# Graph network with expert layers: row sums to three tables, pair adds moved, more key codes joined

## The chip, the cores and the metric

The kernel runs on one core of a Trainium2 chip. The metric is the device time of one execution in microseconds. Three executions of the kernel before took 6115.59 to 6121.12 us, median 6119.78.

## The reference

A table x of 2500 nodes by 256 features passes through eight residual blocks, each on a layer norm of x: an edge network (GIN) with edge features, an expert layer, a graph convolution, an expert layer, a convolution with attention, an expert layer routed by attention over a second graph, an attention block over the first graph, and a last expert layer. The edges of the first list (42500) and of the second (131072) are given as index arrays.

```python
# first block
msg = relu(x[src] + edge_attr @ We + be)          # 42500 x 256
agg = segment_sum(msg, dst, num_segments=2500)
out = (x + agg) @ W + b                           # then batch norm, relu
# graph convolution
out = segment_sum((x @ W)[src] * norm[:, None], dst)
# sixth block
e = leaky_relu(a_src[src] + a_dst[dst]); ee = exp(e - segment_max(e, dst)[dst])
```

## The kernel before, in words

The five compute and queue programs (SP loads, PE, DVE, ACT, POOL) are written out by hand, with semaphores between them. SP, PE, ACT and DVE go through the stages together: each ends a stage in `stage_end` and goes on when all four are there. POOL has no stages. It runs `edges_pool` and then `pairs_pool` straight through, and is tied to the others by semaphores only.

The sums over edges are made in two ways. The first block adds rows: the edges of the first list are taken in K1 = 340 tiles of 125. For tile k POOL gathers the source rows from DRAM (`gather`, L809), PE multiplies the edge features and adds the gathered rows (L632), ACT takes the relu, DVE builds a matrix that sums the tile's edges of equal target (L725), PE multiplies by it (L599), ACT keeps the result (L669), and POOL adds its rows to a table in DRAM by an indirect DMA with addition (`add`, L822). Two edges of a tile with one target are summed before, so an indirect add never meets a row twice; adds to the same table must not be in flight together. So there are two tables, `sums[k % 2]`, and the add of k waits until that of k − 2 has landed. Eight gathers run ahead. The last column of the table counts the degree.

The other blocks use a dense count table of 2500 x 2500 pairs. Each tile of edges is added to it by an indirect DMA of one element per lane (`add_pair`, L760): 340 adds for the first list (table `pairs1`), 1024 tiles of 128 for the second (two tables `pairs2`, the adds alternate between them in portions). Before a tile can be added, DVE compares its keys with those of a super-tile of four tiles (`key1_codes`, L527) so that only one edge of each key in it adds, with the count. For the second list (`key2_codes`, L545) p counts pairs of super-tiles, eight tiles each. Where `joined(p)` holds, each tile is compared over all eight (1024 wide), and the eight are added to one table as one portion. Where it doesn't, each half is compared by itself (512 wide) and portions are of four. A portion waits until the earlier adds to its table have landed.

In the edges stage DVE and PE work in 85 groups of GR = 4 tiles, and every group also codes one super-tile of the first list and, from group 1 on, one pair p of the second (`pairs_of`: groups 20, 40, 60 and 80 have two), up to p = 87. The rest are coded in the first expert stage. So p = 16 falls in group 17, p = 32 in group 32 and p = 53 in group 52.

The order of POOL's work is: adds and gathers in turn for k = 0 to 339, and from k = FIRST1 = 112 (group 28) on EARLY1 = 132 pair adds of the first list spread evenly among them (L835). Then `pairs_pool`: four adds of the first list and two of the second in turn until the first is done, then the rest of the second.

SP, in the edges stage (`edges_sp`), zeroes `sums`, then the tails of the pair tables, then loads the edge features group by group (L560) with a portion of the pair tables' zeroing behind each, and 36 parameter loads (L660) after group 79. The gin stage (`gin_sp`, L850) waits for all row sums, loads both tables back in five blocks, and DVE adds them (L870, L871). SP waits for the whole first list (`pairs_added`) before the table loads of the first graph convolution, and for the whole second list (`pairs2_added`) before those of the sixth block; the stage ahead of the latter stores expert outputs (`outs_e`).

```python
sp.wait_ge(sem("pairs_added"), 16 * K1)          # first gate
table_sp(sp, "l1g", pairs1)
...
for c in range(2):                               # second gate
    sp.wait_ge(sem(f"pairs2_added{c}"), 16 * ADDED2[c])
nbmax_ahead(sp, "l2h", pairs2)
```

Of the kernel before, what the change touches and what calls it, by code (L numbers as in the profile page):

```python
# [22 lines left out]
ALU = mybir.AluOpType  # L23
# [4 lines left out]
N, D = 2500, 256  # L28
P, T = 125, 20
E1, K1 = 42500, 340  # L30
# [8 lines left out]
AGG = D + 1  # L39
# [4 lines left out]
RANK = 1024  # L44
GR = 4
SUPER = 4


LOCAL = 40
# [5 lines left out]
def build(nc, a, out):  # L55
    ctx = ExitStack()
    with ctx:
# [3 lines left out]
        def dram(name, shape, dt=F32):  # L61
            return nc.dram_tensor(name, shape, dt, kind="Internal").ap()
# [7 lines left out]
        def sem(name):  # L70


            if name.startswith(ACROSS):
                if name not in sems:
                    sems[name] = ctx.enter_context(nc.semaphore(name))
                return sems[name]
            names = sems.setdefault(here[0], [])
            if name not in names:
                names.append(name)
            return local[names.index(name)]  # L80
# [6 lines left out]
        WORK = sb("WORK", [128, 10240])  # L87
# [26 lines left out]
        GAT = [sb(f"GAT{i}", [P, T, 4]) for i in range(8)]  # L114

        x_table = dram("x_table", [N, D])
        sums = [dram(f"sums{c}", [N + 128, AGG]) for c in range(2)]
        PAIR_OF = 2 * SUPER
        pairs1 = dram("pairs1", [PAIRS + 128 * PAIR_OF, 1])
        pairs2 = [dram(f"pairs2_{c}", [PAIRS + 128 * PAIR_OF, 1]) for c in range(2)]  # L120
# [61 lines left out]
        LOADED = 32  # L182
        LANES = (slice(0, 112), slice(112, P))

        def spread(sp, name, dst, src):

            for lanes in LANES:
                sp.dma_start(dst[lanes], src[lanes], allow_slow_non_contiguous=True).then_inc(sem(name), 16)  # L188
# [309 lines left out]

        def joined(p):

            return 16 <= p < 32 or 54 <= p < 106

        def key1_rows(pe, g):
            for part in range(3):
# [46 lines left out]
        def edges_sp(sp):  # L551
            sp.dma_start(WE[0:ED], a["L0_gnn_We"]).then_inc(sem("we_loaded"), 16)
            sp.dma_start(WE[ED:ED + 1], a["L0_gnn_be"].rearrange("(e d) -> e d", e=1)).then_inc(sem("we_loaded"), 16)
            zeros = [(table, f"zeroed{1 if table is pairs1 else 2}", at)
                     for table in (pairs1, *pairs2) for at in range(ZP)]

            def group(g):
                if g >= 2:
                    sp.wait_ge(sem("edge_added"), GR * (g - 1))
                sp.dma_start(EA_T[0:ED, g % 2, :], a["edge_t"][:, g * GR * P:(g + 1) * GR * P]  # L560
                             ).then_inc(sem(f"ea_loaded{g % 2}"), 16)

            def zero(table, name, at):
                sp.dma_start(table[0:PAIRS, :].rearrange("(r p q f) o -> r p q (f o)", r=ZP, p=ZL, q=5)[at],
                             ZERO[0:ZL, 0:PAIRS // (ZP * ZL) // 5].unsqueeze(1).to_broadcast([ZL, 5, PAIRS // (ZP * ZL) // 5])
                             ).then_inc(sem(name), 16)

            group(0)
            sp.wait_ge(sem("cleared_zero"), 1)
            for c in range(2):  # L570
                spread(sp, f"zeroed_sums{c}", sums[c][0:N, :].rearrange("(q p r) d -> p q (r d)", p=P, r=10),
                       ZERO[:, 0:10 * AGG].unsqueeze(1).to_broadcast([P, 2, 10 * AGG]))
                sp.dma_start(sums[c][N:N + 128, :].rearrange("(a p) d -> p a d", p=64),
                             ZERO[0:64, 0:2 * AGG].rearrange("p (a d) -> p a d", d=AGG)
                             ).then_inc(sem(f"zeroed_sums{c}"), 16)
            for table in (pairs1, *pairs2):
                sp.dma_start(table[PAIRS:PAIRS + 128 * PAIR_OF, :].rearrange("(p a) o -> p (a o)", p=64),
                             ZERO[0:64, 0:2 * PAIR_OF]).then_inc(sem("zeroed1" if table is pairs1 else "zeroed2"), 16)
            for g in range(1, NG):
                group(g)  # L580
                done = 3 * ZP - len(zeros)
                due = -(-3 * ZP * g // (NG - 6))
                for _ in range(min(due - done, len(zeros))):
                    zero(*zeros.pop(0))
                if g == NG - 6:
                    params(sp)
            assert not zeros
            stage_end(sp)
# [73 lines left out]
        def edges_act(act):  # L662
            act.wait_ge(sem("cleared_sums"), 1)

            def keep(k):
                act.wait_ge(sem("edge_sums"), k + 1)
                if k >= 8:
                    act.wait_ge(sem(f"rows_added{k % 2}"), 16 * ((k - 8) // 2 + 1))
                act.activation(SUMMED[0:P, k % 8, :], PS[0:P, 4 + k % 2, 0:AGG], ACT.Copy).then_inc(sem("sum_kept"), 1)  # L669

            for k in range(K1):
                act.wait_ge(sem("edge_added"), k + 1)
                if k >= 2:
                    act.wait_ge(sem("edge_sums"), k - 1)
                act.activation(MSG[0:P, k % 2, 0:D], PS[0:P, 2 + k % 2, 0:D], ACT.Relu).then_inc(sem("msg_ready"), 1)  # L675
                if k:
                    keep(k - 1)
            keep(K1 - 1)
            stage_end(act)
# [74 lines left out]
            finish(NG - 1, True)  # L754
            stage_end(dve)

        FIRST1, EARLY1 = 112, 132

        def add_pair(pool, table, done, idx, cnt, n):
            pool.indirect_dma_start(table, bass.IndirectOffsetOnAxis(idx[:, n:n + 1], 0), cnt[:, n:n + 1], None,  # L760
# [36 lines left out]
        def edges_pool(pool):  # L797
            pool.memset(ZERO[:, 0:PAIRS // (ZP * ZL)], 0.0).then_inc(sem("cleared_zero"), 1)
            pool.wait_ge(sem("cleared_zero"), 1)
            pool.memset(SUMMED[96:128], 0.0).then_inc(sem("cleared_sums"), 1)  # L800
            pool.wait_ge(sem("cleared_sums"), 1)
            pool.memset(EA_T[64:65], 1.0).then_inc(sem("cleared_ones"), 1)
            pool.wait_ge(sem("t0_stored"), NC * LOADED)

            def gather(k):

                if k >= 8:
                    pool.wait_ge(sem("edge_added"), k - 7)
                pool.indirect_dma_start(GATH[:, k % 8, :], None, x_table,  # L809
                                        bass.IndirectOffsetOnAxis(SRCI[:, k:k + 1], 0)  # L810
                                        ).then_inc(sem(f"gathered{k % 8}"), 16)

            def add(k):
                c = k % 2
                pool.wait_ge(sem("sum_kept"), k + 1)
                if k < 2:
                    pool.wait_ge(sem(f"zeroed_sums{c}"), LOADED + 16)
                if k % GR == 0:
                    pool.wait_ge(sem("rows_coded"), k // GR + 1)
                if k >= 2:  # L820
                    pool.wait_ge(sem(f"rows_added{c}"), 16 * (k // 2))
                pool.indirect_dma_start(sums[c], bass.IndirectOffsetOnAxis(SROW[:, k:k + 1], 0),  # L822
                                        SUMMED[:, k % 8, :], None, compute_op=ALU.add
                                        ).then_inc(sem(f"rows_added{c}"), 16)

            for k in range(8):
                gather(k)
            pairs = 0
            for k in range(K1):
                add(k)  # L830
                if k + 8 < K1:
                    gather(k + 8)
                if k == FIRST1:
                    pool.wait_ge(sem("zeroed1"), 16 * (ZP + 1))
                for n in range(pairs, max(0, EARLY1 * (k + 1 - FIRST1) // (K1 - FIRST1))):  # L835
                    add_pair1(pool, n)
                    pairs += 1
            assert pairs == EARLY1
# [5 lines left out]
        SUMS = [Y[:, 0:T * AGG], flat(ROWS[0:P].rearrange("p a b -> p (a b)"), T * D, T * AGG)]  # L844
        SUMS_T = [v.rearrange("p (t d) -> p t d", d=AGG) for v in SUMS]
        four = lambda c: slice(4 * c, 4 * c + 4)

        def gin_sp(sp):
            for c in range(2):
                sp.wait_ge(sem(f"rows_added{c}"), 16 * K1 // 2)  # L850
            for n in range(NC):
                for c in range(2):
                    spread(sp, f"gin_sums{n}", SUMS_T[c][:, four(n)],
                           sums[c][0:N, :].rearrange("(t p) d -> p t d", p=P)[:, four(n)])
            sp.wait_ge(sem("params_loaded"), 16 * N_PARAMS)
            stage_end(sp)

        def gin_dve(dve):

            st = Steps(dve, "gin_steps")  # L860
# [5 lines left out]
                    st.go(dve.bn_stats(BN[:, m, c * 6:(c + 1) * 6], O0[:, m, c * CH:(c + 1) * CH]))  # L866

            for c in range(NC):
                dve.wait_ge(sem(f"gin_sums{c}"), 2 * LOADED)
                st.step(dve.tensor_tensor(SUMS_T[0][:, four(c)], SUMS_T[0][:, four(c)], SUMS_T[1][:, four(c)], ALU.add))  # L870
                dve.tensor_tensor(XN[:, four(c)], XN[:, four(c)], SUMS_T[0][:, four(c), 0:D], ALU.add  # L871
                                  ).then_inc(sem("gin_in"), 1)
                if c >= 2:
                    stats(c - 2)
# [1868 lines left out]
```

## Time and profile before

| what | value |
| --- | --- |
| three runs, median | 6119.78 us |
| profiled execution, span | 6109.5 us |
| PE busy | 4932.3 us (81%) |
| DVE busy | 3794.6 us (62%) |
| POOL busy | 3155.8 us (52%) |
| ACT busy | 1630.4 us (27%) |
| L760 (pair adds) | 1364 of 1576 ns |
| L822 (sum adds) | 340 of 1562 ns |
| L809 (gathers) | 340 of 1008 ns |

The span reaches from the first to the last instruction; what the device time has beyond it lies before and after. The profile has no time of its own for the profiled execution beside the span. Busy shares are means over stages with different limits, and issuing of DMAs by SP is not counted as busy. An idle time of 0.30 us with the releaser "issue" is one in which the profile shows nothing that the engine waited for.

### The profile page before, as it was taken

Reading aid. Unit: us, or ns where it says so; the run is one execution under the profiler, and the core shown is the slowest. Engines: PE = TensorE matmul, PEld = TensorE weight load, DVE = VectorE, ACT = ScalarE, POOL = GpSimd, SP = SyncE. Lnnn points to the kernel's source line nnn. Section 1 sums busy time; section 2 is a strip of 40 time slices with the busy share of each in tenths; the row PEclk is TensorE's granted clock in tenths of the full one; section 3 lists DMA queues with packets and bytes.
Section 4 is the critical chain, followed back from the end, with each engine's and each line's share of the span. In section 5 each row is a group of like instructions: output and inputs, shape, how many; then the busy total and the mean of one; then the engine's idle time right before and its main releaser. Section 6 shows DMA issues by size and latency. Waiting matters only on the chain.

```text
span 6109.5 us, 70270 instructions
## 1 busy us (share of the span) xinstructions
PE 4932.3 (81%) x23497; PEld 2951.4 (48%) x23497; DVE 3794.6 (62%) x7229; ACT 1630.4 (27%) x2765; POOL 3155.8 (52%) x2151
## 2 busy tenths in 40 slices
PE   5766666656889898989668979777766999999999
PEld 3444444434445575557566656673223333222266
DVE  6797668876676602130234520699996998777744
ACT  2111111112112201220122222127772002666521
POOL 5678888888888888888877877002220000000000
PEclk8878777777999998999877879889998999999999
DMA  7776666665444595559798866884433011222200
GB/s 191 153 143 137 122 128 122 129 96 63 6 11 18 18 125 33 16 7 125 83 191 89 90 51 72 175 174 121 112 102 74 29 29 28 82 81 82 79 11 28
DMA packets 558594, 523.44 MB, mean 86 GB/s; under 512 B 263641, under 2 KB 489874, under 8 KB 557159
## 3 DMA queue, kind: packets, MB, share of 16 engines
q1 hardware_dynamic: 295560, 427.91, 31.5%
q0 software_dynamic: 261696, 90.13, 23.7%
q8 instruction: 164, 2.69, 0.2%
q14 instruction: 146, 1.20, 0.1%
q10 hardware_dynamic: 1028, 1.52, 0.1%
HBM read 365.58 MB, written 153.75 MB: 85 GB/s over the span
## 4 chain that ended last, share of the span: by engine, by line
PE 52%; DVE 18%; issue 9%; SPq 7%; DMA 7%; POOL 6%; ACT 1%; DVEq 0%; ACTq 0%; POOLq 0%; PEldq 0%
SPq L188 6%; PE PS L2390 6%; PE PS L1448 6%; PE PS L1057 6%; PE PS L2227 5%; PE PS L1029 5%; DVE WORK L2031 4%; DVE MXS L2268 4%; PE PS L1754 3%; PE PS L1040 3%; DVE XT L545 3%; POOL sums L822 3%; DVE ROWS L545 2%; DMA WORK<-x_table,WORK 2%; PE PS L1254 2%
## 5 line engine op out<-in xcount | busy, mean ns | idle before, releaser
L760 POOL DMA_INDIRECT pairs<-PAIR_CNT,PAIR_IDX x1364 | 2150.1, 1576 | 491.2 <-issue 453.4
L545 DVE SCALAR_TENSOR_TENSOR XT<-PS,ROWS 128x1024 f32<-128x1024 f32 (+1 forms) x704 | 694.0, 1050 | 160.1 <-PE PS L515 159.7
L822 POOL DMA_INDIRECT sums<-WORK,XT x340 | 531.2, 1562 | 169.3 <-issue 100.8
L2461 DVE SCALAR_TENSOR_TENSOR WORK<-WORK 125x1000 f32<-125x1000 f32 x400 | 462.3, 1197 | 151.1 <-ACT WORK L2429 150.4
L632 PE MATMUL PS<-WORK,IDENT 125*125 125x256 f32 x680 | 277.3, 497 | 272.7 <-DMA WORK<-x_table,WORK 272.4
L2227 PE MATMUL PS<-ROWS 32*125 32x500 f32 x3200 | 451.0, 633 | 28.9 <-DVE MXS L2268 19.3
L2268 DVE TENSOR_REDUCE MXS<-PS 125x4 f32<-125x2000 f32 x200 | 438.9, 2236 | 24.1 <-PE PS L2248 20.0
L2019 POOL TENSOR_TENSOR WORK<-WORK,ROWS 125x500 f32<-125x500 f32 x100 | 126.0, 1260 | 630.8 <-ACT WORK L1983 630.8
L2429 ACT ACTIVATE WORK<-PS 125x1000 f32<-125x1000 f32 x400 | 380.0, 1002 | 237.8 <-PE PS L2378 237.8
L675 ACT ACTIVATE WORK<-PS 125x256 f32<-125x256 f32 x340 | 131.0, 385 | 1155.0 <-PE PS L632 1155.0
L515 PE MATMUL PS<-ROWS 128*128 128x512 bf16 x768 | 265.6, 471 | 212.0 <-DVE XT L545 154.3
L1057 PE MATMUL PS<-WORK 128*125 128x256 f32 x1760 | 408.7, 387 | 3.7 <-ACT WORK L1126 3.7
L809 POOL DMA_INDIRECT WORK<-x_table,WORK x340 | 342.8, 1008 | 127.8 <-issue 87.8
L1029 PE MATMUL PS<-XT,WORK 128*128 128x500 f32 x880 | 394.5, 592 | 5.4 <-DVE X L1109 2.1
L1705 DVE CUSTOM_DVE_ANT_0 ROWS<-ROWS 125x1250 f32<-125x1250 f32 x200 | 281.0, 1458 | 189.6 <-ACT ROWS L1691 189.5
L1162 DVE SCALAR_TENSOR_TENSOR X<-PS,G,X 125x256 f32<-125x256 f32 x280 | 122.9, 479 | 443.3 <-PE PS L1057 442.9
L1057 PEld LDWEIGHTS PS<-WORK 128*125 128x125 f32 x1760 | 338.6, 193 | 90.8 <-issue 37.1
L1448 PE MATMUL PS<-Y,WORK 125*125 x1600 | 356.0, 386 | 6.7 <-DMA WORK<-pairs 6.7
L1671 PE MATMUL PS<-IDENT,WORK 125*125 125x125 f32 x1920 | 259.2, 305 | 123.0 <-ACT ROWS L1691 63.8
L1448 PEld LDWEIGHTS PS<-Y,WORK 125*125 125x125 f32 x1600 | 306.3, 192 | 61.0 <-issue 13.4
L632 PEld LDWEIGHTS PS<-WORK,IDENT 125*125 125x125 f32 x680 | 150.1, 240 | 357.2 <-DMA WORK<-x_table,WORK 333.6
L527 DVE SCALAR_TENSOR_TENSOR ROWS<-PS,WORK,XT 125x500 f32<-125x500 f32 x340 | 230.7, 735 | 137.9 <-PE PS L505 137.8
(338 smaller groups left out, 8134.3 us busy)
## 6 DMA issues: line engine op xcount, KB each, us to landing
WORK<-pairs SPq DMA_DIRECT2D x400, 218.8 KB
pairs<-ROWS SPq DMA_DIRECT2D x75, 976.6 KB, 7.4
WORK<-pairs SPq DMA_DIRECT2D x48, 1093.8 KB
WORK<-pairs SPq DMA_DIRECT2D x80, 546.9 KB
pairs<-PAIR_CNT,PAIR_IDX POOLq DMA_INDIRECT x1364
WORK<-pairs SPq DMA_DIRECT2D x40, 382.8 KB
XT<-pairs SPq DMA_DIRECT2D x12, 1093.8 KB
mask_t<-ROWS SPq DMA_DIRECT2D x40, 273.4 KB
```

Source lines behind the costliest of these rows:

```text
L188: sp.dma_start(dst[lanes], src[lanes], allow_slow_non_contiguous=True).then_inc(sem(name), 16)
L545: dve.scalar_tensor_tensor(junk[:, slot:slot + width // SUPER, :].rearrange("p a n -> p (a n)"), PS[:, bank + (0 if both else h):bank + (2 ...
L632: pe.matmul(PS[0:P, 2 + k % 2, 0:D], IDENT[0:P, 0:P], GATH[0:P, k % 8, :], start=False, stop=True).then_inc(sem("edge_added"), 1)
L760: pool.indirect_dma_start(table, bass.IndirectOffsetOnAxis(idx[:, n:n + 1], 0), cnt[:, n:n + 1], None, compute_op=ALU.add).then_inc(sem(do ...
L822: pool.indirect_dma_start(sums[c], bass.IndirectOffsetOnAxis(SROW[:, k:k + 1], 0), SUMMED[:, k % 8, :], None, compute_op=ALU.add).then_inc ...
L1029: ins = pe.matmul(PS[:, m, 0:CH], w1[:, k, m * 128:(m + 1) * 128], XT[:, k, c * CH:(c + 1) * CH], start=k == 0, stop=k == 1)
L1057: ins = pe.matmul(PS[0:P, 6 + j // 2, (j % 2) * D:(j % 2 + 1) * D], h, w3[:, k, :], start=k == 0, stop=k == kk - 1)
L1448: ins = pe.matmul(sums_of(j), TABLE_IN[u][0:P, j * P:(j + 1) * P], Y256[:, ds(i * TABLES + u, 1), :], start=False, stop=False, skip_group_ ...
L2227: ins = pe.matmul(PS[0:P, banks[g], 0:CH], HT[group(g), m, t * P:(t + 1) * P], HT[group(g), m, c * CH:(c + 1) * CH], start=True, stop=last)
L2268: dve.tensor_reduce(MXS[:, at:at + G4], PS[0:P, b:b + G4, 0:CH], AX, ALU.max).then_inc(sem("l3m_read"), 1)
L2429: act.activation(E3[q % 8], PS[0:P, b:b + 2, 0:CH], ACT.Exp, scale=float(DH) ** -0.5).then_inc(sem("l3a_exp"), 1)
L2461: dve.scalar_tensor_tensor(E3[q % 8], E3[q % 8], 1.0, A3[n % 4][0:P].unsqueeze(1).to_broadcast([P, 2, CH]), ALU.min, ALU.mult).then_inc(se ...
```

## The change

There are three tables of row sums instead of two, taken in turn; all three are zeroed at the start, and gin reads and adds three. For blocks 3 and 4 of the third table SP waits until the buffer's former block is summed. 96 instead of 132 pair adds of the first list are spread among the edges, from the same tile on; the other 36 follow in `pairs_pool`. The pairs p = 32 to 53 of the second list are joined too.

```diff
--- before.py
+++ after.py
@@ -44,6 +44,7 @@
 RANK = 1024
 GR = 4
 SUPER = 4
+N_SUMS = 3
 
 
 LOCAL = 40
@@ -114,7 +115,7 @@
         GAT = [sb(f"GAT{i}", [P, T, 4]) for i in range(8)]
 
         x_table = dram("x_table", [N, D])
-        sums = [dram(f"sums{c}", [N + 128, AGG]) for c in range(2)]
+        sums = [dram(f"sums{c}", [N + 128, AGG]) for c in range(N_SUMS)]
         PAIR_OF = 2 * SUPER
         pairs1 = dram("pairs1", [PAIRS + 128 * PAIR_OF, 1])
         pairs2 = [dram(f"pairs2_{c}", [PAIRS + 128 * PAIR_OF, 1]) for c in range(2)]
@@ -498,7 +499,7 @@
 
         def joined(p):
 
-            return 16 <= p < 32 or 54 <= p < 106
+            return 16 <= p < 106
 
         def key1_rows(pe, g):
             for part in range(3):
@@ -567,7 +568,7 @@
 
             group(0)
             sp.wait_ge(sem("cleared_zero"), 1)
-            for c in range(2):
+            for c in range(N_SUMS):
                 spread(sp, f"zeroed_sums{c}", sums[c][0:N, :].rearrange("(q p r) d -> p q (r d)", p=P, r=10),
                        ZERO[:, 0:10 * AGG].unsqueeze(1).to_broadcast([P, 2, 10 * AGG]))
                 sp.dma_start(sums[c][N:N + 128, :].rearrange("(a p) d -> p a d", p=64),
@@ -665,7 +666,7 @@
             def keep(k):
                 act.wait_ge(sem("edge_sums"), k + 1)
                 if k >= 8:
-                    act.wait_ge(sem(f"rows_added{k % 2}"), 16 * ((k - 8) // 2 + 1))
+                    act.wait_ge(sem(f"rows_added{(k - 8) % N_SUMS}"), 16 * ((k - 8) // N_SUMS + 1))
                 act.activation(SUMMED[0:P, k % 8, :], PS[0:P, 4 + k % 2, 0:AGG], ACT.Copy).then_inc(sem("sum_kept"), 1)
 
             for k in range(K1):
@@ -754,7 +755,7 @@
             finish(NG - 1, True)
             stage_end(dve)
 
-        FIRST1, EARLY1 = 112, 132
+        FIRST1, EARLY1 = 112, 96
 
         def add_pair(pool, table, done, idx, cnt, n):
             pool.indirect_dma_start(table, bass.IndirectOffsetOnAxis(idx[:, n:n + 1], 0), cnt[:, n:n + 1], None,
@@ -811,14 +812,14 @@
                                         ).then_inc(sem(f"gathered{k % 8}"), 16)
 
             def add(k):
-                c = k % 2
+                c = k % N_SUMS
                 pool.wait_ge(sem("sum_kept"), k + 1)
-                if k < 2:
+                if k < N_SUMS:
                     pool.wait_ge(sem(f"zeroed_sums{c}"), LOADED + 16)
                 if k % GR == 0:
                     pool.wait_ge(sem("rows_coded"), k // GR + 1)
-                if k >= 2:
-                    pool.wait_ge(sem(f"rows_added{c}"), 16 * (k // 2))
+                if k >= N_SUMS:
+                    pool.wait_ge(sem(f"rows_added{c}"), 16 * (k // N_SUMS))
                 pool.indirect_dma_start(sums[c], bass.IndirectOffsetOnAxis(SROW[:, k:k + 1], 0),
                                         SUMMED[:, k % 8, :], None, compute_op=ALU.add
                                         ).then_inc(sem(f"rows_added{c}"), 16)
@@ -844,13 +845,16 @@
         SUMS = [Y[:, 0:T * AGG], flat(ROWS[0:P].rearrange("p a b -> p (a b)"), T * D, T * AGG)]
         SUMS_T = [v.rearrange("p (t d) -> p t d", d=AGG) for v in SUMS]
         four = lambda c: slice(4 * c, 4 * c + 4)
+        SUMS_3 = [flat(WORK, 6200 + u * 4 * AGG, 4, AGG)[0:P] for u in range(3)]
 
         def gin_sp(sp):
-            for c in range(2):
-                sp.wait_ge(sem(f"rows_added{c}"), 16 * K1 // 2)
+            for c in range(N_SUMS):
+                sp.wait_ge(sem(f"rows_added{c}"), 16 * len(range(c, K1, N_SUMS)))
             for n in range(NC):
-                for c in range(2):
-                    spread(sp, f"gin_sums{n}", SUMS_T[c][:, four(n)],
+                if n >= 3:
+                    sp.wait_ge(sem("gin_in"), n - 2)
+                for c in range(N_SUMS):
+                    spread(sp, f"gin_sums{n}", SUMS_T[c][:, four(n)] if c < 2 else SUMS_3[n % 3],
                            sums[c][0:N, :].rearrange("(t p) d -> p t d", p=P)[:, four(n)])
             sp.wait_ge(sem("params_loaded"), 16 * N_PARAMS)
             stage_end(sp)
@@ -866,8 +870,9 @@
                     st.go(dve.bn_stats(BN[:, m, c * 6:(c + 1) * 6], O0[:, m, c * CH:(c + 1) * CH]))
 
             for c in range(NC):
-                dve.wait_ge(sem(f"gin_sums{c}"), 2 * LOADED)
+                dve.wait_ge(sem(f"gin_sums{c}"), N_SUMS * LOADED)
                 st.step(dve.tensor_tensor(SUMS_T[0][:, four(c)], SUMS_T[0][:, four(c)], SUMS_T[1][:, four(c)], ALU.add))
+                st.step(dve.tensor_tensor(SUMS_T[0][:, four(c)], SUMS_T[0][:, four(c)], SUMS_3[c % 3], ALU.add))
                 dve.tensor_tensor(XN[:, four(c)], XN[:, four(c)], SUMS_T[0][:, four(c), 0:D], ALU.add
                                   ).then_inc(sem("gin_in"), 1)
                 if c >= 2:
```

## Rows read from the trace of the kernel before

**Rows 1.** The page: span, and slices of POOL.
```profile
span 6109.5 us, 70270 instructions
...
POOL 5678888888888888888877877002220000000000
```

**Rows 2.** Busy time by stretch (start:end length, then busy us per engine).
```profile
50.00:286.00 236.00, 171.23 (x584) 116.03 (x584) 161.61 (x620) 43.58 (x132) 163.29 (x128) 0.80 0.75 164
...
850.00:1290.00 440.00, 293.78 (x910) 186.15 (x909) 368.06 (x988) 67.98 (x206) 358.92 (x267) 0.75 0.67 125
```

**Rows 3.** Groups of POOL, 850 to 1290 us (busy, mean ns | idle before).
```profile
L822 POOL DMA_INDIRECT sums<-WORK,XT x104 | 161.7, 1555 | 31.7 <-issue 29.0 <-ACT WORK L669 2.1 <-DVE XT L734 0.3
L809 POOL DMA_INDIRECT WORK<-x_table,WORK x103 | 104.6, 1015 | 31.4 <-issue 25.6 <-PE PS L632 4.3 <-DMA sums<-WORK,XT 1.5
L760 POOL DMA_INDIRECT pairs<-PAIR_CNT,PAIR_IDX x60 | 93.7, 1562 | 18.3 <-issue 17.7 <-DMA sums<-WORK,XT 0.3 <-DVE PAIR_IDX L687 0.3
```

**Rows 4.** Timeline of DVE, edges (start us, us, what).
```profile
398.37 0.34 DVE L725 SCALAR_TENSOR_TENSOR WORK<-PS,WORK 125x125 f32<-125x125 f32 x1
...
485.55 0.34 DVE L725 SCALAR_TENSOR_TENSOR WORK<-PS,WORK 125x125 f32<-125x125 f32 x1
...
1396.80 1.28 DVE L545 SCALAR_TENSOR_TENSOR XT<-PS,ROWS 128x1024 f32<-128x1024 f32 x1
...
1398.01 1.28 DVE L545 SCALAR_TENSOR_TENSOR XT<-PS,ROWS 128x1024 f32<-128x1024 f32 x1
```

**Rows 5.** Groups of DVE by form, 560 to 840 us.
```profile
L545 DVE SCALAR_TENSOR_TENSOR XT<-PS,ROWS 128x512 f32<-128x512 f32 x136 | 93.7, 747 | 49.8 <-PE PS L515 49.6
```

**Rows 6.** Source line 822 (the sum adds), 50 to 286 us.
```profile
  issue: 29.0, 44
  DMA sums<-WORK,XT: 16.8, 10
...
DMA to landing us min/median/max: 3.8/4.4/6.7
```

**Rows 7.** Timeline, start of the edges, SP and POOL.
```profile
51.82 1.61 POOL L822 DMA_INDIRECT sums<-WORK,XT  x1 [10.00 <-issue]
...
57.47 1.46 SPq L560 DMA_DIRECT2D WORK<-in_edge_t  x1
...
64.66 1.58 POOL L822 DMA_INDIRECT sums<-WORK,XT  x1 [9.92 <-DMA sums<-ROWS]
```

**Rows 8.** Timeline, end of the edges.
```profile
1322.24 59.32 SPq L560 DMA_DIRECT2D WORK<-in_edge_t  x5
...
1417.63 0.16 DVE L695 SCALAR_TENSOR_TENSOR PAIR_IDX<-ROWS,SPARES 128x8 int32<-128x8 f32 x1
...
1420.46 1.54 POOL L822 DMA_INDIRECT sums<-WORK,XT  x1 [0.30 <-issue]
...
1424.28 0.84 SPq L188 DMA_DIRECT2D Y<-sums  x2
```

**Rows 9.** Gin: a stretch as in rows 2, and DVE's timeline.
```profile
1424.00:1450.00 26.00, 12.98 (x49) 8.21 (x50) 12.20 (x12) 7.32 (x18) 18.70 (x11) 0.68 1.07 198
...
1430.86 1.23 DVE L870 TENSOR_TENSOR Y<-Y,ROWS 125x1028 f32<-125x1028 f32 x1 [13.07 <-DMA ROWS<-sums]
```

**Rows 10.** Waits on POOL, 2290 to 2616 us (us in total, times, longest).
```profile
POOL pairs L760 <- DMA pairs<-PAIR_CNT,PAIR_IDX: 8.9, 7, 2.8
```

**Rows 11.** Timeline at the two gates.
```profile
2120.17 5.44 SPq L188 DMA_DIRECT2D WORK<-pairs  x8
...
3817.21 1.54 POOL L760 DMA_INDIRECT pairs<-PAIR_CNT,PAIR_IDX  x1 [0.30 <-issue]
...
3841.01 7.72 SPq L188 DMA_DIRECT2D outs_e<-ROWS  x4
...
3851.78 15.53 SPq L188 DMA_DIRECT2D WORK<-pairs  x8
```

## The prediction

> **What bounds the kernel now.** I read the page first, then a table by stage, then each queue. The page gives a span of 6109.5 us [rows 1]; the median of the runs shown is 6119.8, 10.3 above it. The sum is made in the span's times and its difference is taken off the median. A measurement of this kernel tells 0.2% (12 us) from no change. The page shows POOL at 7 or 8 tenths for over half of the span and then idle: its indirect transfers run in one string that ends at 3817 us [rows 1, 11]. In the edges, between 850 and 1290 us, POOL is busy 358.9 of 440 us. That is saturation, because every issue is followed by 0.30 us put down to "issue" [rows 2, 3].
>
> So from tile k = 112 on a tile costs POOL a sum add (1.555 + 0.30), a gather (1.015 + 0.30) and 132/228 of a pair add (1.562 + 0.30) [rows 3]: 3.17 + 1.08 = 4.25 us, 17.0 per group of four. Check: 104 tiles in 440 us are 4.23 each. DVE is under that: where it paced the kernel, six groups of joined codes took from 398.37 to 485.55 us, 14.5 each [rows 4]. Before k = 68 no pair is joined, and POOL sets the pace with waits of its own: 64 sum adds in 236 us, 3.69 per tile against 3.17 [rows 2, 6]. Groups 17 to 27 (joined, still without pair adds) go at DVE's 14.5 against POOL's 12.7.
>
> After the edges two gates tie the other engines to POOL. SP needs the first list before the load at 2120.17, and the whole second list before the load at 3851.78. POOL issues its last pair add at 3817.21. The nearest row for a landing, that of sum adds, has a median of 4.4 us, so it is over at 3822; SP's last stores of the stage before are issued until 3848.7 [rows 6, 11]. **The second gate has 30 us of slack, and on that number this change turns.**
>
> **36 pair adds out of the edges.** Each is 1.86 us, 36 make 67 us. On POOL nothing is saved: they come later in the same string. For the other engines the edges end sooner, as long as POOL stays the bound: a tile costs 3.17 + 96/228 × 1.86 = 3.95 us, a group 15.8, against DVE's 14.5 in every group from 28 on, since groups 32 to 52 are joined as well. Groups 40, 60 and 80 code two pairs, 8 × 1.21 = 9.7 us more (a 1024-wide code starts 1.21 us after the one before) [rows 4]. POOL does not starve on that: up to seven sums are kept and not yet added, 7 × 3.95 = 28 us of work, and DVE recovers 1.3 us a group. At the end it is tight. SP issues the 36 parameter loads and only then, from 1322 us, the last edge loads; DVE ends at 1417.8, the last sum add is issued at 1420.46, and gin's first load at 1424.28 [rows 8]. DVE's tail does not shrink, POOL's last 35 tiles do by 35 × 0.29 = 10 us, so some 5 of the 67 us are lost upstream, and POOL idles some 3 us (0 to 10).
>
> **The third table, waits.** A sum add now waits for the add three before it, not two. Up to 286 us POOL waited 16.8 us for sum adds in 10 places (13.8 over the usual 0.30). "Issue" holds 29.0 in 44 places, of which 13.2 is the usual and 9.7 the first add; the other 6 may be the same wait [rows 6, 7]. In three turns of 3.17 an add has 9.5 us to land, and the longest took 6.7 [rows 6]. I take 18 us (0 to 20). What stands between 286 and 468 us lies under DVE's pace and gives nothing.
>
> **The third table, zeroing.** 2500 × 257 × 4 bytes = 2.57 MB more are zeroed on SP's queue ahead of group 1's edge load. With two tables that load is issued at 57.47, and the add of k = 1, which waits for the second table's zeros, comes 12.8 us after that of k = 0, at 64.66 [rows 7]. I take 13 us (9 to 18) for all engines, before k = 2 and group 1. Net at the start: 18 − 13 = 5 us gained, on POOL too.
>
> The page DMA: Bandwidth & Descriptors of the Trainium skill, section Bandwidth, gives some 358 GB/s between SBUF and HBM for a core, by which the zeros would be an estimated 7 us and the final gain 6 us more. The row has 12.8 for the same size, and that stands in the sum.
>
> **The third table, reading.** Gin loads 2.57 MB more, in 30 transfers instead of 20. From 1424 to 1450 us the DMA engines were full (share 1.07) at 198 GB/s: 13 us. DVE adds once more per block, 1.23 us, of which the last is on the path [rows 9]. 14 us (10 to 18), hidden where POOL's gate binds later. SP's new wait before blocks 3 and 4 is for a block summed long before; queued behind it are only those blocks' own loads.
>
> **22 pairs joined.** On DVE 22 × 8 × (1.28 − 0.75) = 93 us more, which goes under POOL's pace as above: in 280 us of these groups DVE had stood 50 us for PE's rows at the 512-wide codes alone [rows 4, 5]. On POOL eight adds, not four, go to a table in turn, so one waits for adds eight back. These pairs pass POOL at about 2290 to 2616 us, where it waited 8.9 us in 7 places for pair adds, 6.8 over the usual [rows 10]. I take 6 us (−5 to 10).
>
> **The sum.** Upstream 67 − 5 + 5 − 14 = 53 us earlier at both gates. First gate: SP is ready at 2067. POOL leaves the edges at about 1353 with 244 adds of the first list and, two to every four, 122 of the second: 366 × 1.85 = 677 us, with some waits 2036, landed 2041. It does not bind. Second gate: SP is ready at 3852 − 53 = 3799. POOL is through at 3822 − 5 (start) − 6 (joined) + 3 (tail) = 3814. **POOL is 15 us late and becomes the gate**, so the reading of a third table costs nothing at the end. Gain 3852 − 3814 = 38: 6119.8 − 38 = **6082 us**. What is late next is the string of pair adds itself.
>
> **Rivals.**
> 1. *POOL ends sooner*: 20 us of waits gone, zeros at 9, 10 from joining: 3822 − 21 = 3801. Gain 51, 6069; the upstream path (59 earlier) is then hardly under it. For it: POOL has other long waits after 2616 us that may move. Against: those go with bursts of loads, which stay. Chance 0.13.
> 2. *The third table buys no waits*: landings lengthen with three in flight, since DMA is at a share of 0.75 there [rows 2]. POOL then ends at 3822 + 13 − 6 + 3 = 3832: gain 20, 6100. Against: the longest landing of 6.7 us. Chance 0.13.
> 3. *DVE and POOL hinder each other* in groups 28 to 84, now 1.3 us apart, not 2.5 or more: POOL idles 25 us beyond the 3, which goes straight to the gate: gain 13, 6107. Against: in groups 17 to 27 the two were 1.8 apart and kept DVE's pace. Chance 0.10.
> 4. *Slower*: groups 32 to 52, once joined, run well over 14.5, PE's rows and DVE's codes waiting for each other in turn. POOL's idle outweighs the gain once it exceeds 38 us in 21 groups: from a period of 17.6 us. At 20 us it is 21 × 4.2 = 88, and the kernel 50 slower, 6170. Against: groups from 53 on have this form and keep POOL saturated at 17.0 [rows 3]. Chance 0.05.
> 5. *The gate isn't where I see it*, the slack being used by something that no row shows: gain under 12, 6114. Chance 0.04.
>
> **Numbers.** Forecast 6082 with 0.55. Faster (below 6107.5): 0.55 + 0.13 + 0.13 and most of the third, 0.88. Same 0.07, slower 0.05. The range 6062 to 6103 takes in rivals 1 and 2 and the forecast's own bounds: the start from −9 − 9 to +6, joining from −11 to +4, the tail ±5.
>
> **What would show it.** The edges end near 1357 us, with tiles at 3.95 us; the add of k = 2 near 78 us; no sum add waiting for sum adds; DVE at 14 to 15 us a group in 32 to 52; gin 13 us longer. The first load of the second list comes at about 3814, behind pair adds and not behind stores. It is wrong if that load follows its predecessor's stores at once (the upstream path binds), or if POOL stands for ACT's kept sums in groups 28 to 84 (rivals 3 and 4).

## The result, and the profile after

The changed kernel takes 6081.7 us in the median of four executions (6070.9 to 6086.5), the kernel before 6120.5 (6115.6 to 6122.6): a ratio of 0.9937, interval 0.9923 to 0.9950. That is 39 us less. The profiled execution is the longest of the four, 6086.5 us with a span of 6084.7; against the profiled span of before it is only 24.8 us less. So a device time is about 1.8 us above its span, and most of the 10.3 us between the span of before and its median was chance: if the same 1.8 us hold there, the profiled execution of before lay 8 to 9 us under its median. Sizes of steps below are read from traces, sizes of kernels from medians.

The page of the changed kernel, span, busy time and the slices of POOL and DVE:

```profile
span 6084.7 us, 70288 instructions
...
PE 4877.0 (80%) x23497; PEld 2929.9 (48%) x23497; DVE 3893.7 (64%) x7234; ACT 1631.9 (27%) x2765; POOL 3158.7 (52%) x2151
...
DVE  6899999974766302120325511689996998777744
...
POOL 5868888878888878888888878102220000000000
```

POOL does the same 3157 us or so of work. DVE has 99 us more: 93 for the 176 codes that are 1024 instead of 512 wide, 6 for gin's five further adds. It sits at 9 tenths in six slices of the edges. Line numbers after are one higher than before in this part (L823 for L822, L761 for L760), five higher further down.

The start, in the changed kernel's timeline (the rows that answer to [rows 7]):

```profile
47.91 5.39 SPq L189 DMA_DIRECT2D sums<-ROWS  x2
...
64.92 2.25 SPq L561 DMA_DIRECT2D WORK<-in_edge_t  x1
...
65.45 1.58 POOL L823 DMA_INDIRECT sums<-WORK,XT  x1 [11.81 <-DMA sums<-ROWS]
...
75.68 1.59 POOL L823 DMA_INDIRECT sums<-WORK,XT  x1 [7.36 <-DMA sums<-ROWS]
...
81.05 1.57 POOL L823 DMA_INDIRECT sums<-WORK,XT  x1 [2.49 <-ACT WORK L670]
```

The zeros of the third table hold the add of k = 2 to 75.68 us and group 1's edge load to 64.92. The add of k = 3 is at 81.05; in the kernel before it was at 72.09, so it is 9 us late:

```profile
72.09 1.57 POOL L822 DMA_INDIRECT sums<-WORK,XT  x1 [1.37 <-ACT WORK L669]
```

Then the waits are gone. The sum adds of the changed kernel from 50 to 286 us, against [rows 6] (us in all, number of waits):

```profile
  DMA sums<-ROWS: 19.2, 2
  ACT WORK L670: 6.4, 14
  DMA sums<-WORK,XT: 0.9, 3
```

Three idle times of 0.3 us are left of the ten waits for sum adds. From k = 3 to k = 68 POOL takes 206.7 us, 3.18 per tile; before it took 233.2. The pace with pair adds, groups of POOL in the changed kernel from 850 to 1210 us (against [rows 3]):

```profile
L823 POOL DMA_INDIRECT sums<-WORK,XT x91 | 141.6, 1556 | 27.7 <-issue 23.5 <-ACT WORK L670 4.0 <-DVE XT L735 0.3
L810 POOL DMA_INDIRECT WORK<-x_table,WORK x91 | 92.3, 1015 | 27.7 <-issue 23.8 <-PE PS L633 2.7 <-DMA sums<-WORK,XT 0.6
L761 POOL DMA_INDIRECT pairs<-PAIR_CNT,PAIR_IDX x38 | 59.3, 1561 | 11.6 <-issue 11.0 <-DMA sums<-WORK,XT 0.3 <-DVE XT L735 0.3
```

91 tiles in 360 us are 3.96 each, and nobody else ended POOL's idle times for long. The end of the edges and both gates, in the changed kernel's timeline (against [rows 8, 11]):

```profile
1344.79 1.54 POOL L823 DMA_INDIRECT sums<-WORK,XT  x1 [0.30 <-issue]
...
1346.82 0.16 DVE L696 SCALAR_TENSOR_TENSOR PAIR_IDX<-ROWS,SPARES 128x8 int32<-128x8 f32 x1
...
1348.61 0.84 SPq L189 DMA_DIRECT2D Y<-sums  x2
...
2062.85 188.02 SPq L189 DMA_DIRECT2D WORK<-pairs  x80
...
3697.58 102.22 SPq L189 DMA_DIRECT2D outs_e<-ROWS  x18
...
3823.50 1.54 POOL L761 DMA_INDIRECT pairs<-PAIR_CNT,PAIR_IDX  x1 [0.30 <-issue]
...
3829.86 16.40 SPq L189 DMA_DIRECT2D WORK<-pairs  x8
```

Gin starts 75.7 us earlier, the first gate is passed 57.3 us earlier. At the second gate the stores now end at 3799.8 instead of 3848.7, and the load used to follow them 3 us later; it follows 30 us later here, 6.4 us after the last pair add was issued. POOL has become the gate.

### The profile page after: what moved, and what is told of

Its sections match the earlier page's. It is cut to its first block, busy times and chain, and to the rows that moved or that the text cites. A ratio compares the mean times of both kernels' runs of the same rounds, so it can differ in the third digit from the quotient of the medians.

```text
span 6084.7 us, 70288 instructions
## 1 busy us (share of the span) xinstructions
PE 4877.0 (80%) x23497; PEld 2929.9 (48%) x23497; DVE 3893.7 (64%) x7234; ACT 1631.9 (27%) x2765; POOL 3158.7 (52%) x2151
## 4 chain that ended last, share of the span: by engine, by line
POOL 30%; PE 25%; DVE 18%; issue 15%; DMA 6%; SPq 5%; ACT 1%; DVEq 0%; ACTq 0%; POOLq 0%
POOL pairs L761 29%; DVE XT L546 7%; PE PS L2395 6%; PE PS L2232 5%; SPq L189 4%; DVE WORK L2036 4%; DVE MXS L2273 4%; DMA pairs<-PAIR_CNT,PAIR_IDX 4%; PE PS L1062 2%; PE PS L516 2%; PE PS L1034 2%; PE PS L2253 2%; DMA WORK<-x_table,WORK 2%; PE PS L633 1%; DVE WORK L2042 1%
## 5 line engine op out<-in xcount | busy, mean ns | idle before, releaser
L761 POOL DMA_INDIRECT pairs<-PAIR_CNT,PAIR_IDX x1364 | 2152.9, 1578 | 503.1 <-issue 468.3
L546 DVE SCALAR_TENSOR_TENSOR XT<-PS,ROWS 128x1024 f32<-128x1024 f32 (+1 forms) x704 | 786.7, 1184 | 98.6 <-PE PS L516 98.3
L823 POOL DMA_INDIRECT sums<-WORK,XT x340 | 531.5, 1563 | 160.4 <-issue 90.2
L516 PE MATMUL PS<-ROWS 128*128 128x512 bf16 x768 | 282.8, 496 | 386.4 <-DVE XT L546 328.8
L516 PEld LDWEIGHTS PS<-ROWS 128*128 128x128 bf16 x768 | 80.5, 115 | 533.4 <-DVE XT L546 357.6
L1453 PEld LDWEIGHTS PS<-Y,WORK 125*125 125x125 f32 x1600 | 305.9, 192 | 65.2 <-issue 17.8
L1676 PEld LDWEIGHTS PS<-IDENT,WORK 125*125 125x125 f32 x1920 | 246.7, 214 | 164.8 <-issue 89.0
L633 PE MATMUL PS<-WORK,IDENT 125*125 125x256 f32 x680 | 250.6, 456 | 67.1 <-DMA WORK<-x_table,WORK 67.0
```

The source lines that it names most:

```text
L516: ins = pe.matmul(PS[:, bank, :], PICK[:, s % 128:s % 128 + 1].to_broadcast([128, 128]), upper(KEY2_ROWS[s // 128][:, part, :]), start=par ...
L546: dve.scalar_tensor_tensor(junk[:, slot:slot + width // SUPER, :].rearrange("p a n -> p (a n)"), PS[:, bank + (0 if both else h):bank + (2 ...
L1453: ins = pe.matmul(sums_of(j), TABLE_IN[u][0:P, j * P:(j + 1) * P], Y256[:, ds(i * TABLES + u, 1), :], start=False, stop=False, skip_group_ ...
L1676: ins = pe.matmul(PS[0:P, 3 * b + j // 4, j % 4 * P:(j % 4 + 1) * P], bufs[m % len(bufs)][c][0:P, j, b * P:(b + 1) * P], IDENT[0:P, 0:P], ...
```

## The experiments

Eleven kernels ran, e1 to e4, e5 to e8 and e9 to e11 on a chip each; the kernel before, run beside them, took 6113.2, 6119.4 and 6128.6 us. Ratios are to that, and only ratios are compared across chips. They are the ratios on record with each run, and differ from the quotient of the two medians by up to 0.0015 (in e1, where the quotient is 0.9903). The table has, from each trace, the issue of the last sum add and of the last pair add, the time at which SP could have loaded (end of the stores plus 3.05 us) and the first load behind the second gate.

| run | ratio (interval) | last sum add | last pair add | SP ready | load |
| --- | --- | --- | --- | --- | --- |
| before | 1 | 1420.5 | 3817.2 | 3851.8 | 3851.8 |
| changed | 0.9937 (0.9923 to 0.9950) | 1344.8 | 3823.5 | 3802.8 | 3829.9 |
| e1 changed, last 40 out | 0.9888 (0.9867 to 0.9910) | 1346.1 | 3740.9 | 3796.2 | 3796.2 |
| e2 132 among the edges | 0.9991 (0.9979 to 1.0004) | 1409.4 | 3829.1 | 3863.0 | 3863.0 |
| e3 two tables | 0.9970 (0.9957 to 0.9983) | 1381.0 | 3841.7 | 3817.3 | 3847.9 |
| e4 p = 32 to 53 in halves | 0.9934 (0.9915 to 0.9953) | 1348.4 | 3819.8 | 3782.3 | 3825.5 |
| e5 changed again | 0.9932 (0.9909 to 0.9954) | 1345.4 | 3823.2 | 3800.3 | 3829.1 |
| e6 before, last 40 out | 0.9993 (0.9981 to 1.0005) | 1426.2 | 3758.6 | 3862.0 | 3862.0 |
| e7 before with 96 | 0.9960 (0.9943 to 0.9978) | 1374.2 | 3844.8 | 3797.6 | 3850.5 |
| e8 two zeroed in setup | 0.9918 (0.9899 to 0.9937) | 1338.3 | 3814.7 | 3793.1 | 3820.9 |
| e9 joined from 54 | 0.9939 (0.9926 to 0.9953) | 1322.7 | 3840.1 | 3796.6 | 3846.1 |
| e10 e9, one zeroed in setup | 0.9934 (0.9920 to 0.9948) | 1315.8 | 3812.9 | 3788.8 | 3819.4 |
| e11 e8 and e9 | 0.9907 (0.9894 to 0.9921) | 1314.7 | 3817.4 | 3791.2 | 3823.9 |

**Is POOL's string the gate?** e1 takes the last 40 pair adds from the changed kernel, e6 from the kernel before; the tables of the second list then lack these 40 tiles.

```diff
-            for n in range(n2, K2):
+            for n in range(n2, K2 - 40):
...
-                pool.wait_ge(sem(f"pairs2_added{c}"), 16 * ADDED2[c])
+                pool.wait_ge(sem(f"pairs2_added{c}"), 16 * (ADDED2[c] - 20))
```

> The changed kernel with the last 40 pair adds of the second list left out (so the two tables of the second list lack 40 tiles); everything else as in the changed kernel. Theory (the string of POOL's transfers is the gate of the sixth block): POOL is through 74 us sooner, and the load of the second list goes directly behind the stores of the stage before, which in the changed kernel's trace end 27 to 30 us ahead of it. 6055 us, 22 to 30 less than the changed kernel. Rival (the engines ahead of the gate set the time, the gate only looks late): no change, 6078 to 6085.

> The kernel before with the last 40 pair adds of the second list left out. Theory: there the gate has 30 us of slack and POOL does not hold it, so taking 74 us from POOL's end changes nothing: the same as the kernel before within 0.2%. Rival (the gate was already POOL's in most executions): 10 to 30 us faster.

e1 took 6053.8 us, 0.9888; e6 6119.5 us, 0.9993. The same 74 us of POOL's work are worth 0.4 to 0.5% behind the change (24 us against e4, which ran on the same chip) and nothing ahead of it. e1 in its timeline, the last pair add and the load:

```profile
3740.93 1.54 POOL L761 DMA_INDIRECT pairs<-PAIR_CNT,PAIR_IDX  x1 [0.30 <-issue]
...
3796.24 14.80 SPq L189 DMA_DIRECT2D WORK<-pairs  x8
```

55 us pass between them: the gate has gone back to the engines, and the gain ends at their time. In e6 the load comes 103 us behind the last pair add:

```profile
3758.64 1.54 POOL L760 DMA_INDIRECT pairs<-PAIR_CNT,PAIR_IDX  x1 [0.30 <-issue]
...
3862.02 15.34 SPq L188 DMA_DIRECT2D WORK<-pairs  x8
```

The theory stands, the rivals fall.

**Which part brought it?** e2 puts the 36 adds back, e3 the third table, e4 the joining; e7 is the kernel before with the 36 adds moved alone.

```diff
-        FIRST1, EARLY1 = 112, 96
+        FIRST1, EARLY1 = 112, 132          # e2
-N_SUMS = 3
+                                           # e3: two tables, all lines on the third undone
-            return 16 <= p < 106
+            return 16 <= p < 32 or 54 <= p < 106          # e4
```

> The changed kernel with 132 instead of 96 pair adds of the first list among the edges. Theory: the edges end 67 us later for all engines, POOL's string is as long as before and ends where it did, so the engines are the later ones at the gate: 6120 to 6130 us, no better than the kernel before, since gin's third table then costs its 14 us in the open. Rival (the third table and the joining bring the gain, not the moved adds): 6080 to 6100.

> The changed kernel with two tables of row sums instead of three (96 pair adds among the edges and the joining kept). Theory: POOL waits again for sum adds in the first 286 us (+18) and has 8 to 13 us less of zeroing to wait for, gin is 14 us shorter but hides behind POOL's gate: 6084 to 6092. Rival A (the third table carries the gain): over 6100. Rival B (it is worth nothing, its zeroing eats all): 6074 to 6082.

> The changed kernel with p = 32 to 53 not joined, as in the kernel before. Theory: POOL waits some 6 us more for pair adds when these pass it (2250 to 2600 us), which goes straight to the gate: 6085 to 6092. Rival A (joining is worth nothing to POOL): 6080 to 6084. Rival B (the wider codes of DVE hold POOL up in groups 32 to 52): 6065 to 6078, with fewer waits of sum adds for ACT's kept sums.

> The kernel before with 96 pair adds among the edges and nothing else changed. Theory: with two tables the sum adds wait for each other also beyond k = 112 once the pace rises, as in the run with two tables and the joining (14 us between k = 128 and 304), so the edges end near 1380 us, and POOL ends some 20 us later than in the kernel before or at 3840: 6095 to 6108, 0.1 to 0.3% under the kernel before. Rival (the moved adds alone carry the gain): 6078 to 6085.

e2 took 6109.8 us, the same as before (6113.2). Its load behind the gate comes 34 us after the last pair add: the engines hold it, as expected, so without the moved adds there is no gain. The absolute figure was expected at least 10 us too high; 7 us of that are the chip, since it was reckoned from the first.

e7 took 6093.7 us, 0.9960, just past the lower bound of what was expected (6095, 0.3%). e3 took 6097.6 us, 0.9970. That is nearly 6 us over what I expected as it stands; counted from its own chip's kernel before, 0.9970 would be 6102 us on the first chip, which is where rival A (the third table carries the gain) puts it. So rival A is half right: the moved adds without the third table are worth 0.3 to 0.4%, and the third table brings the other 0.2 to 0.4% (20 us between e3 and e4 on one chip, 13 us between e7 and e5 on another; both pairs also differ in the joining, which e4 shows to be worth little). I had put it at little. Neither of the two does it alone, since e2, with the third table and all adds among the edges, gains nothing.

Where the table works is seen in the waits of POOL from 470 to 1290 us (us in all, number, longest). e3:

```profile
POOL sums L822 <- ACT WORK L669: 19.0, 28, 3.2
POOL sums L822 <- DMA sums<-WORK,XT: 6.0, 5, 2.7
```

and the changed kernel:

```profile
POOL sums L823 <- ACT WORK L670: 12.3, 28, 4.0
...
POOL sums L823 <- DMA sums<-WORK,XT: 0.9, 3, 0.3
```

From k = 128 to 304 the changed kernel takes 697.9 us, e3 711.9 and e7 711.1 (the wait of 4.0 us is behind this stretch, at k = 323): once the tiles come every 3.95 us, two tables are short here too, by 14 us, joined or not. At 4.25 us per tile they had been enough, and before I read that as needing nothing.

e4 took 6077.5 us, 0.9934, which its interval does not tell from the changed kernel. I had expected 6085 to 6092, and that is not what came: by its ratio e4 lies with rival A, by its microseconds with rival B, which holds that the wide codes cost POOL time in groups 32 to 52. B's mechanism isn't there, for from k = 112 to 339 e4 takes 896.8 us, e5 896.7 and the changed kernel 894.7. POOL's waits from 2290 to 2616 us did move as expected. First the changed kernel, against the 8.9 us of [rows 10], then e4:

```profile
POOL pairs L761 <- DMA pairs<-PAIR_CNT,PAIR_IDX: 0.9, 3, 0.3
```

```profile
POOL pairs L761 <- DMA pairs<-PAIR_CNT,PAIR_IDX: 5.5, 5, 3.2
```

Joining these 22 pairs saves about 5 us of waits in the trace, and that is under what the medians can tell.

**Is the rest chance?**

> The changed kernel itself, so that the other runs can be set against it on the same chip. The gate of the sixth block should again be held by pair adds, and the ratio to the kernel before should be 0.993 to 0.995. Its trace shows how much of the idle time in POOL's string after the edges (133.6 us over 1.848 us per transfer in the changed kernel's trace, 118.2 in that of before) is chance: theory, 115 to 140.

e5 took 6080.6 us (6056.4 to 6096.4), 0.9932. Idle time in POOL's string over 1.848 us per transfer was 132.6 us, as expected. Over all traces it lies between 116 and 141 us where the pairs from 16 on are joined, with or without 32 to 53. So a difference of 15 us between two single traces in this string is no finding.

**Towards a better version.** If POOL's string is the gate, what starts it sooner or shortens it should come through. e8 zeroes two tables in the setup stage, behind the loads of x.

```diff
         def setup_sp(sp):
             ...
+            sp.wait_ge(sem("cleared_zero"), 1)
+            for c in range(2):
+                zero_sums(sp, c)
             for c in range(NC):
                 sp.wait_ge(sem("ln0_norm"), 4 * c + 4)
...
-            for c in range(N_SUMS):
+            for c in range(2, N_SUMS):
+                zero_sums(sp, c)
```

> The changed kernel with the first two tables of row sums zeroed in the setup stage, behind the loads of x; the third is zeroed where all three were. Theory: POOL's start is the gate's start; k = 2 and group 1 wait only for the third table's zeros, near 62 to 68 us instead of 76, and each us goes through to the end: 8 to 14 us under the changed kernel, 6068 to 6074. Rival (the zeros delay the stores of the normalised x, on which the first gather waits, by as much): the same as the changed kernel or up to 5 us slower.

e8 took 6070.2 us, 0.9918, 10 us under e5 on the same chip, as expected; but the intervals of the two overlap, so the medians alone don't show the gain. The stores of the normalised x do come later, so the first gather is issued at 45.19 instead of 31.09 us and the add of k = 0 at 63.1; but those of k = 2 and 3 at 69.5 and 72.7, 6 and 8 us sooner than in the changed kernel, and POOL stays ahead by that (the last sum add 6.5 us sooner, the last pair add 9).

e9 leaves only p = 54 to 105 joined, e10 and e11 add one or two tables zeroed in the setup stage.

```diff
-            return 16 <= p < 106
+            return 54 <= p < 106
```

> The changed kernel with only p = 54 to 105 joined (16 to 53 in halves). Theory: in groups 17 to 27 DVE's wide codes held POOL up by 17 us (k = 68 to 112, 162 us for 44 tiles where POOL needs 140), and that idle time goes straight to the gate; without it POOL reaches the end 15 to 20 us sooner, less some 5 to 10 us of waits for pair adds when p = 16 to 53 pass it in portions of four: 6068 to 6076, 5 to 12 us under the changed kernel. Rival (the joining saves POOL as much as it costs): the same as the changed kernel within 4 us.

> e9 with the first table zeroed in the setup stage, the other two where they were. Theory: the stores of the normalised x are held up by half of the 14 us that two tables cost, k = 2 comes near 67 to 70 us: 3 to 8 us under e9, 6062 to 6072. Rival (only what is behind the last table's zeros counts): as e9.

> e9 with two tables zeroed in the setup stage (e8 and e9 together). Theory: both savings lie in POOL's string at different places and add up, since the engines are still 15 us or more ahead of the gate: 8 to 12 us under e9, 6056 to 6066, about 1% under the kernel before. Rival (the gate passes to the engines): 6066 to 6072.

e9 took 6093.5 us, 0.9939: no gain, the rival's case. Yet the theory was right on the first half. The sum adds from 286 to 468 us waited 25.2 us for ACT's kept sums in the changed kernel, behind DVE's wide codes:

```profile
  ACT WORK L670: 25.2, 14
```

and in e9 there is this:

```profile
  ACT WORK L670: 2.4, 8
```

k = 112 is reached 24 us sooner. All of it is given back later, with interest. POOL's waits from 2007 to 2760 us, first the changed kernel, then e9:

```profile
POOL pairs L761 <- DMA pairs<-PAIR_CNT,PAIR_IDX: 1.2, 4, 0.3
```

```profile
POOL pairs L761 <- DMA pairs<-PAIR_CNT,PAIR_IDX: 37.5, 21, 4.8
```

The reason is where the pairs pass. e9 by stretch (busy us of PE, PEld, DVE, ACT and POOL; the last three columns are the granted clock, the DMA share and GB/s):

```profile
2040.00:2230.00 190.00, 179.63 (x757) 145.91 (x756) 4.01 (x10) 0.00 (x0) 138.25 (x91) 0.92 0.98 128
2290.00:2616.00 326.00, 309.87 (x959) 184.51 (x960) 59.71 (x139) 80.82 (x122) 263.50 (x172) 0.95 0.58 16
```

By the count of transfers, p = 17 to 27 are added between 2045 and 2230 us, while SP loads the first list for the graph convolution and the DMA engines are at 0.98; 27.4 of the 37.5 us fall between 2040 and 2230. There four adds (7.4 us) are too short a time for a landing, and eight are enough. From 2290 us on the engines carry little (16 GB/s), and p = 32 to 53 pass with 8.1 us of waits. So joining pays here by the traffic at the time of the adding, not by the number of pairs.

e10 took 6089.9 us, 0.9934, 3.6 us under e9, at the low end of what was expected and too little for the intervals to tell. e11 took 6075.7 us, 0.9907, 17.8 us under e9, which is more than the 8 to 12 expected, and 53 under the kernel before. Against the kernel before, both it and e8 are clearly faster; against the changed kernel neither is shown to be, since both intervals overlap that of e5 (e11's lies just under that of the changed kernel's first runs). That two savings add up in e11 isn't shown either, for e9 by itself saved nothing, and which of e8 and e11 is better stays open. In both the load still comes 28 to 33 us after SP is ready, so POOL is still the gate.

## Why the prediction was right

The range, the sign and the mechanism held; that 6082 met 6081.7 is luck, as the step on POOL's end shows. Step by step:

- *The second gate has 30 us of slack and takes over.* Right, and shown by e1, e2 and e6. In the traces the load is 27 to 29 us behind SP's readiness (changed, e5), 15 were predicted. Where POOL is the gate, the load follows the last pair add by 5.7 to 6.5 us; the 4.4 us taken from sum adds were some 2 short.
- *36 adds are 67 us for the engines and nothing for POOL.* Right: 3.96 us per tile against 3.95, 697.9 us from k = 128 to 304 against 750.0. The tail lost its 5 us (k = 304 to 339: 139.6 before, 134.2 after, 10 had POOL alone counted).
- *The third table, waits: 18 us.* Mis-sized: 26.5 us between k = 3 and 68, above the upper bound of 20. The bound held the 13.8 us named and 6 us of "issue" up to 286 us. Left out were 5.4 us more of the same waits in group 16, which is not joined and reaches to 305 us (k = 64 and 67, below), and 1.8 us put down to ACT. "What stands between 286 and 468 us lies under DVE's pace" began one group too early. A further 14 us from k = 128 on belong to it (e3, e7); there the table does not gain over before, it keeps the faster pace possible. I had left that out.
- *Zeroing 13 us.* 9 us, the lower bound. By the page DMA: Bandwidth & Descriptors of the Trainium skill, section Bandwidth, with its limit of 358 GB/s to HBM, it would have been an estimated 7 us. The row had 12.8, and the measured 9 lies between them. In gin the row was right, as the step on gin shows.
- *What lies under DVE's pace gives nothing.* DVE held groups 17 to 27 harder than before: k = 68 to 112 took 162.4 us instead of 156.4, so 6 of the 17.6 us won by k = 68 (287.7 us against 305.3) were lost again.
- *Gin 14 us.* From gin's first load to the first gate it takes 708 to 718 us in the nine traces with three tables, 696 to 700 in the four with two: 15 us.
- *Joining 6 us.* 5 to 8 us in the waits of that stretch, nothing that medians show (e4).
- *POOL through at 3814.* Not in this trace: the last pair add was issued at 3823.5, 6 us later than before, where 3810 was expected. The edges were left 9 us sooner than POOL's moved work explains (2 were expected), but the string after them had 133.6 us of idle time where before had 118.2. This is the step that was wrong in kind: I took the waits of one trace as fixed but for those that I moved. Of the 15.4 us, 10 lie in the regular gaps that the last section describes (51 us in eight of them, 41 in seven before). The load behind the gate thus came at 3829.9 and not at 3814, 16 us late.
- *Gain 38 us.* Between the two traces the gate came 21.9 us earlier, what follows it was 2.9 us shorter, and that is the 24.8 us of the spans. The other 14 of the 39 us come from which executions were profiled: that of before 9 us under its median, that of the changed kernel 5 us above. That these 14 and 3 us made up for the 16 is luck. (In e6, whose profiled execution lies 7 us above its median, SP is ready at 3862 and not at 3852.)

The two waits for sum adds behind 286 us, in the kernel before:

```profile
289.38 1.58 POOL L822 DMA_INDIRECT sums<-WORK,XT  x1 [2.42 <-DMA sums<-WORK,XT]
...
302.15 1.57 POOL L822 DMA_INDIRECT sums<-WORK,XT  x1 [3.56 <-DMA sums<-WORK,XT]
```

Rivals: 1 (POOL sooner, engines the bound) and 5 did not occur; 2 fell with the pace of 3.18 us per tile (in e3, with two tables, k = 3 to 68 take 234.7 us again); 3 and 4 fell with POOL's unbroken pace in groups 28 to 84.

## What to carry to other kernels

Where one queue runs through all stages and only its last item is waited for, look for the slack at that wait before anything else: here 30 us of it decided that moving 67 us of work gives 39. Once that queue is the gate, engine time ahead of it is free as long as it doesn't hold the queue up (as DVE did in groups 17 to 27), and work can be judged by what it saves the queue alone; the wider comparison on DVE paid only for items that pass while the DMA engines are full. And when a pace is raised, count again whether the number of buffers that sufficed at the old pace (two tables at 4.25 us per tile) still does.

## What the runs showed of the hardware

Not expected was a regular stall in POOL's string of indirect transfers. Every 112 transfers one gap is longer, put down to "issue"; it is seen from the 478th transfer after the last sum add on. In the changed kernel's timeline:

```profile
2246.98 1.54 POOL L761 DMA_INDIRECT pairs<-PAIR_CNT,PAIR_IDX  x1 [0.30 <-issue]
2257.17 1.54 POOL L761 DMA_INDIRECT pairs<-PAIR_CNT,PAIR_IDX  x1 [8.64 <-issue]
```

```profile
2885.62 1.54 POOL L761 DMA_INDIRECT pairs<-PAIR_CNT,PAIR_IDX  x1 [0.31 <-issue]
2895.82 1.54 POOL L761 DMA_INDIRECT pairs<-PAIR_CNT,PAIR_IDX  x1 [8.65 <-issue]
```

Between them lie two more, of 3.54 and 2.35 us, so the four are each 112 transfers apart. In this trace the eight cost 2 to 10 us each beyond the usual 0.30, together 51 us. They stand behind the same transfers (the 478th, 590th and so on, counted from the last sum add) in every kernel with 96 adds among the edges, and behind the 530th, 642nd and so on in the three with 132. One place is an exception: in e1, e3 and e10 the gap behind the 1150th is missing, and one transfer earlier stands a wait of 5 to 6 us for a landing. So their places belong to the sequence of POOL's instructions and not to what the other engines do.

Their length goes with the traffic. Of the 56 gaps in seven traces (changed, e4, e5, e7, e8, e9, e11), the 29 in which the DMA engines had a share of 0.51 or less took 2.1 to 5.0 us. Of the 27 with a share of 0.61 or more, all but two (3.3 and 3.7 us) took 6.1 to 11.2 us. What happens in them no run shows; it wasn't tried. The traces record the loading of instructions as packets of their own, and in the changed kernel's trace six of the eight gaps hold none, so that isn't shown to be the cause. The sum of the eight differs from trace to trace between 33 us (e4) and 51 us (changed), and where POOL is the gate nothing behind it makes up for that.
